# Second mixture of a two-layer gated kernel: from all experts for all tokens to rows scattered by expert

## The chip, the cores and the metric

The kernel runs on one core of one Trainium2 chip. The metric is device microseconds of one execution. A core has five engines that each follow a queue of their own and meet at semaphores: TensorE (PE, matrix products into PSUM banks), VectorE (DVE), ScalarE (ACT), GpSimd (POOL) and SyncE (SP, which only issues transfers). ScalarE and GpSimd issue transfers too, and an indirect transfer, whose row numbers come from a table in on-chip memory, is issued by GpSimd.

## The reference, cut to what matters

4096 tokens (64 batches of 64) of 128 values go through two layers. Each layer is a gated cross-attention and a gated mixture of experts:

```
x = x + tanh(g_xattn[0]) * attention0(layernorm(x), ctx, ...)
x = x + tanh(g_ffn[0])   * mixture0(layernorm(x), ...)      # 64 experts of 88, 8 per token, 2 shared
x = x + tanh(g_xattn[1]) * attention1(layernorm(x), ctx, ...)
x = x + tanh(g_ffn[1])   * mixture1(layernorm(x), ...)      # 8 experts of 512, 2 per token
```

The last line is the one that the change rewrites:

```
logits = xf @ Wg                                   # [4096, 8]
top_vals, top_idx = top_k(logits, 2)
gate_w = softmax(top_vals)
comb = sum(gate_w[..., None] * one_hot(top_idx, 8), axis=1)
for ei in range(8):
    hdd = gelu(xf @ W1[ei] + b1[ei])               # [4096, 512]
    y = hdd @ W2[ei] + b2[ei]                      # [4096, 128]
    out = out + comb[:, ei:ei+1] * y
```

All data are float32. Six of the eight weights of a token are zero, so a kernel may compute all eight experts for every token, or only the two that count.

## The kernel before, in words

The program has four stages, and every engine goes through them in the order `attention(0)`, `block_tables()` and `experts()`, `attention(1)`, `mixture(...)`. The order inside a stage is written out by hand.

**Attention** handles 16 groups of four batches (256 tokens, two tiles of 128) as a pipeline: in step j the group j is normalized and projected (`f`), group j-1 gets its scores (`m`), j-2 its values (`v`), j-3 its output projection and residual (`b`), j-4 its routing logits and ranks (`r`), j-5 its routing weights or row numbers (`k`). VectorE takes the maxima, the ranks and the residual, ScalarE the exponentials and the copies out of PSUM, GpSimd the inverse standard deviations (`deviation`, L1553). In layer 1 the routing ends with a table of weights `rw`, turned by TensorE (L599) and kept by ScalarE as `rwT` (L857); the normalized tokens are kept turned as `xn2T` (L910). Step 20 of layer 1 (`late`) runs inside the mixture, after chunk 10 of its first group.

**The first mixture** is sparse already. During attention(0) GpSimd scatters each token's row eight times into a table in DRAM (`expert_rows`), in a section per expert (L1516). TensorE counts the rows of each expert (L611 to L617), and `block_tables` makes the list of blocks of 128 rows: which expert and which rows a block takes. Everything is in two halves of 16 tiles. `experts` does 16 batches for the shared experts and 96 batches of four blocks: SyncE loads four blocks of rows (L409, three buffers), TensorE turns them (L674), multiplies by gate and up weights at an address from a register (L690), ScalarE applies silu, VectorE the product, TensorE turns the hidden values (L699) and multiplies down (L712), ScalarE copies the result (L963) and stores it to `expert_results` in DRAM (L967). GpSimd gathers eight result rows per token (L1531), and VectorE adds them into `x`, one scaled addition each (L1458). The first half's gathers run beside the second half's blocks; the second half's 128 gathers run in attention(1), ten a step, in front of and behind the deviations.

**The second mixture** is dense. It goes through eight groups of 512 tokens, and for each through 32 chunks of 128 hidden units (`group`, L766). Each float32 operand is split in two float32r parts, high and rest, and a product is three matmuls (`split_product`, L735: lines L739, L740, L741). Per chunk: ScalarE makes the high part of the weights (L1000) and GpSimd the rest (L1548); TensorE multiplies up (three matmuls of 512 columns) and spreads the token's weight for this expert over the 128 partitions (L781); ScalarE applies the gelu (L1029); VectorE multiplies by the spread weight (L1491); ScalarE and VectorE split the hidden values (L1007, L1472); TensorE multiplies down, three chunks later (three matmuls of 512 columns), adding up all 32 chunks in one bank. Behind a group, ScalarE copies the sum (L1013), TensorE turns it (L763), VectorE adds it to `x` (L1478) and SyncE stores 512 tokens (L443).

## Time and profile before

| | |
|---|---|
| median of three runs | 1671.78 us (1669.03 to 1679.33) |
| the profiled execution | 1676.6 us |
| its span, first to last instruction | 1674.8 us |
| TensorE busy | 1477.2 us, 88% of the span |
| VectorE, ScalarE, GpSimd busy | 1003.3, 913.8, 827.7 us |
| mean granted TensorE clock | 0.859 of full |
| moved by DMA | 129.98 MB |

The page has the share of busy time of each engine, the same in 40 slices with the granted clock, the chain of work that ended last, and the costliest groups of instructions by line. In such a row, `L712 PE MATMUL bank<-wexp,arena 88*128 x768 | 111.5, 291 | 53.1 <-...` means: line 712, TensorE, what it writes and reads, 768 records, busy for 111.5 us together, 291 ns each on the mean, and 53.1 us of idle time in front of them. A timeline row has the start and the duration in us, the engine, the line, and in brackets the idle time before and what ended it. In a row of stretches each engine has its busy time and its number of instructions.

### The profile page before, as it was taken

Reading aid. Unit: us, or ns where it says so; the run is one execution under the profiler, and the core shown is the slowest. Engines: PE = TensorE matmul, PEld = TensorE weight load, DVE = VectorE, ACT = ScalarE, POOL = GpSimd, SP = SyncE. Lnnn points to the kernel's source line nnn. Section 1 sums busy time; section 2 is a strip of 40 time slices with the busy share of each in tenths; the row PEclk is TensorE's granted clock in tenths of the full one; section 3 lists DMA queues with packets and bytes.
Section 4 is the critical chain, followed back from the end, with each engine's and each line's share of the span. In section 5 each row is a group of like instructions: output and inputs, shape, how many; then the busy total and the mean of one; then the engine's idle time right before and its main releaser. Section 6 shows DMA issues by size and latency. Waiting matters only on the chain. (4 is left out here: it accounts for less than half of the span.)

```text
span 1674.8 us, 30515 instructions
## 1 busy us (share of the span) xinstructions
PE 1477.2 (88%) x9346; PEld 1082.5 (65%) x9346; DVE 1003.3 (60%) x2799; ACT 913.8 (55%) x1981; POOL 827.7 (49%) x910
## 2 busy tenths in 40 slices
PE   4889887698767989966889899979999999999998
PEld 3666665488767988854666666645565565655655
DVE  4677876655334876653555555345666676666666
ACT  3666662245323555535444454446776776777776
POOL 1046667607785377767555540023444444444442
PEclk9999995799778999987655665558999999999999
DMA  6346541426443577753221110000000000000000
GB/s 166 84 111 180 175 143 45 126 83 197 146 137 120 169 212 206 205 157 106 75 68 43 43 41 7 1 0 1 8 1 7 1 6 6 0 7 0 6 7 7
DMA packets 210981, 129.98 MB, mean 78 GB/s; under 512 B 50882, under 2 KB 197378, under 8 KB 210834
## 3 DMA queue, kind: packets, MB, share of 16 engines
q1 hardware_dynamic: 139122, 60.97, 13.3%
q10 hardware_dynamic: 55296, 33.56, 6.8%
q0 software_dynamic: 16416, 33.65, 6.7%
q8 instruction: 72, 1.18, 0.3%
q14 instruction: 75, 0.61, 0.1%
HBM read 67.28 MB, written 60.82 MB: 76 GB/s over the span
## 5 line engine op out<-in xcount | busy, mean ns | idle before, releaser
L1548 POOL TENSOR_TENSOR wring<-weights,wring 128x256 fp32r<-128x256 f32 x256 | 240.8, 941 | 315.7 <-ACT wring L1000 315.7
L1516 POOL DMA_INDIRECT expert_rows<-xn2T,slot x256 | 253.3, 990 | 85.7 <-issue 80.0
L1472 DVE TENSOR_TENSOR hsplit<-work,hsplit 128x512 fp32r<-128x512 f32 x256 | 177.1, 692 | 126.1 <-ACT hsplit L1007 125.4
L1007 ACT ACTIVATE hsplit<-work 128x512 fp32r<-128x512 f32 x256 | 161.2, 630 | 144.9 <-PE bank L741 143.4
L1491 DVE TENSOR_TENSOR work<-work,bank 128x512 f32<-128x512 f32 x256 | 176.0, 687 | 68.5 <-ACT work L1029 52.7
L1029 ACT ACTIVATE work<-bank,b 128x512 f32<-128x512 f32 x256 | 171.5, 670 | 10.4 <-PE bank L741 9.7
L712 PE MATMUL bank<-wexp,arena 88*128 x768 | 111.5, 291 | 53.1 <-DVE arena L1377 52.7
L1531 POOL DMA_INDIRECT late_rows<-expert_results,slot x128 | 124.3, 971 | 59.2 <-issue 35.3
L848 ACT ACTIVATE work<-bank 128x512 f32<-128x512 f32 x128 | 76.5, 598 | 139.6 <-PE bank L507 136.9
L690 PE MATMUL bank<-wexp,arena 128*128 x768 | 147.2, 338 | 0.0
L1531 POOL DMA_INDIRECT xn2T<-expert_results,slot x128 | 121.9, 952 | 38.9 <-issue 38.9
L712 PEld LDWEIGHTS bank<-wexp,arena 88*128 88x128 f32 x768 | 99.8, 203 | 60.4 <-issue 60.3
L739 PE MATMUL bank<-hsplit,wring 128*128 128x512 f32 x256 | 131.9, 515 | 0.9 <-DVE hsplit L1472 0.8
L1555 POOL TENSOR_SCALAR ve<-mv 128x2 f32<-128x2 f32 (+1 forms) x52 | 11.8, 227 | 241.6 <-DVE mv L1143 155.7
L955 ACT ACTIVATE arena<-bank 128x176 f32<-128x176 f32 x224 | 70.1, 317 | 111.7 <-PE bank L690 78.5
L781 PE MATMUL bank<-xin,sel 16*128 16x512 f32 x256 | 130.1, 508 | 0.0
L690 PEld LDWEIGHTS bank<-wexp,arena 128*128 128x128 f32 x768 | 125.0, 204 | 7.3 <-issue 2.3
L507 PE MATMUL bank<-cst,work 128*128 128x128 f32 x512 | 106.7, 345 | 25.6 <-ACT sg L906 17.3
L963 ACT ACTIVATE arena<-bank 128x512 f32<-128x512 f32 x96 | 57.3, 597 | 114.3 <-PE bank L712 84.1
L1377 DVE COPY arena<-bank 88x512 f32<-88x512 f32 x112 | 76.5, 683 | 66.0 <-PE bank L699 65.9
L520 PEld LDWEIGHTS bank<-vm,work 128*64 128x64 f32 x2048 | 89.7, 171 | 36.2 <-ACT work L848 21.2
L781 PEld LDWEIGHTS bank<-xin,sel 16*128 16x128 f32 x256 | 48.1, 188 | 98.0 <-DVE work L1491 72.9
(197 smaller groups left out, 3204.9 us busy)
## 6 DMA issues: line engine op xcount, KB each, us to landing
arena<-expert_rows SPq DMA_DIRECT2D x384, 64.0 KB
expert_results<-arena ACTq DMA_DIRECT2D x96, 256.0 KB
expert_rows<-zero SPq DMA_DIRECT2D x256, 64.0 KB
arena<-in_ctxT ACTq DMA_DIRECT2D x32, 256.0 KB, 2.7
expert_rows<-xn2T,slot POOLq DMA_INDIRECT x256
weights<-in_mix SPq DMA_DIRECT2D x8, 512.0 KB
wexp<-in_mix SPq DMA_DIRECT2D x15, 176.0 KB
x<-in_x SPq DMA_DIRECT2D x4, 512.0 KB, 7.8
```

The lines of the kernel that those rows point to most:

```text
L507: mm = pe.transpose(w[:, bb * P:(bb + 1) * P], work[:, u, bb * P:(bb + 1) * P], ident)
L690: mm = pe.matmul(out[:, b * 2 * I0:(b + 1) * 2 * I0], xgT[:, n % 2, 2 * h + b, :], wflat[:, bass.ds(offsets[m][2 * h + b], 2 * I0)], start ...
L712: mm = pe.matmul(bank[7][:, b * P:(b + 1) * P], hT[0:I0, n % 2, b, :], wflat[0:I0, bass.ds(offsets[m][b] + 2 * I0, P)], start=True, stop=T ...
L739: pe.matmul(out, wh, xh, start=start, stop=False, skip_group_check=True)
L781: pe.matmul(bank[4 + c % 2][:, :], sel[strip, cols:cols + P], xin[strip, u, 2, :], start=True, stop=True).then_inc(S["spread"], 1)
L1007: act.activation(hsplit[:, c % 2, 0, :], work2[:, c % 2, :], ACT.Copy).then_inc(S["h_hi"], 1)
L1029: act.activation(work[:, c % 2, :], bank[c % 2][:, :], ACT.Gelu_apprx_tanh, bias=b1[:, c:c + 1]).then_inc(S["act"], 1)
L1472: dve.tensor_tensor(hsplit[:, c % 2, 1, :], work2[:, c % 2, :], hsplit[:, c % 2, 0, :].bitcast(F32), ALU.subtract).then_inc(S["h_lo"], 1)
L1491: dve.tensor_tensor(held, work[:, c % 2, :], bank[4 + c % 2][:, :], ALU.mult).then_inc(S["hid"], 1)
L1516: pool.indirect_dma_start(xs, bass.IndirectOffsetOnAxis(ap=slot[:, t, k:k + 1], axis=0), xn2all[:, t, :].bitcast(I32), None).then_inc(s_sc ...
L1531: pool.indirect_dma_start(yg[h][:, t // 2 % 2, t % 2, k, :].bitcast(I32), None, ys, bass.IndirectOffsetOnAxis(ap=slot[:, t, k:k + 1], axis ...
L1548: pool.tensor_tensor(wsplits[:, place, 1, 0:CW[1]], weights[:, c * CW[1]:(c + 1) * CW[1]], wsplits[:, place, 0, 0:CW[1]].bitcast(F32), ALU ...
```

## The change

The second mixture is built like the first. What it does, part by part:

- Routing of layer 1 keeps, for each token, which expert is first and which is second (`chosen`) and their two weights (`wk1`, times the gate). TensorE ranks the rows by expert (`rank_rows`, now in both layers), and VectorE makes the row number in the table (`slot1`). The turned weights and the turned tokens are no longer made; the normalized tokens are kept as rows.
- GpSimd scatters each token's row twice (`scatter_late`, 64 indirect transfers) during attention(1), after the gathers of the first mixture.
- SyncE loads the weights with the bias columns beside them, fills unused rows with zeros, and loads 20 batches of four blocks.
- `late_experts`: 80 blocks of 128 rows. VectorE copies a block's up weights and bias to a ring of four places; TensorE makes four plain fp32 products up into one bank; ScalarE applies four gelus of 128 columns; TensorE makes four plain fp32 products down, two blocks later; VectorE adds the bias of the output for four blocks at once; ScalarE stores them.
- GpSimd gathers two rows per token (`gather_late`, 64 indirect transfers), VectorE adds them into `x`, and SyncE stores 512 tokens at a time.
- All 21 steps of attention(1) come before the mixture.

The diff, cut to its core (tables, zero fills and declarations are left out):

```diff
 # SyncE
 def load_mixture():
-    part = CHUNKS[1] * CW[1] // 8
-    for i in range(8):
-        sp.wait_ge(layers[1]["vp"], i + 1)
-        sp.dma_start(weights[:, i * part:(i + 1) * part], A["mix1"][...]).then_inc(s_ffw, 16)
+    for e in range(E1):
+        sp.wait_ge(layers[1]["vp"], e + 1)
+        for a, at in ((0, 0), (1, W2C)):
+            sp.dma_start(wx[:, e, at:at + F1]..., mixed1[:, e, :, a, :]).then_inc(s_ffw, 16)
+    ...
+def load_late_rows(m):
+    if m >= XR:
+        sp.wait_ge(l_xt, m - XR + 1)
+    rows[m] = registers(sp, tabR1, m * NB, NB, (ROWS1 - P) * D)
+    for b in range(NB):
+        sp.dma_start(xg1[:, m % XR, b, :].bitcast(I32), flat1[bass.ds(rows[m][b], P * D)]...).then_inc(s_load[m % XR], 16)
 # TensorE
-if k and L: back_weights()
-if k and L == 0: rank_rows()
+if k: rank_rows()
 ...
-def mixture(step):
-    ...
+def late_experts():
+    def up(i):
+        m = i // NB
+        if i % NB == 0:
+            pe.wait_ge(l_xtc, m + 1)
+            offsets[m] = registers(pe, tabW1, m * NB, NB, (E1 - 1) * W1ROW)
+        pe.wait_ge(l_wc, i + 1)
+        if i > 2:
+            pe.wait_ge(l_act, i - 2)
+        for c in range(FC):
+            mm = pe.matmul(bank[2 + i % 3][:, c * P:(c + 1) * P], wcopy[:, i % WRING, c * P:(c + 1) * P], xgT1[:, m % 2, i % NB, :], ...)
+        mm.then_inc(l_up, 1)
+    def down(i):
+        m, b = i // NB, i % NB
+        pe.wait_ge(l_act, i + 1)
+        if b == 0 and m > 1:
+            pe.wait_ge(l_yc, m - 1)
+        for c in range(FC):
+            mm = pe.matmul(bank[5 + m % 2][:, b * P:(b + 1) * P], hT1[:, i % WRING, c, :],
+                           wxflat[:, bass.ds(offsets[m][b] + (W2C + c * P), P)], start=c == 0, stop=c == FC - 1, ...)
+        mm.then_inc(l_y, 1)
+    turn_rows(0)
+    for i in range(NBLOCKS1):
+        up(i)
+        if i % NB == 1 and i // NB + 1 < RT1:
+            turn_rows(i // NB + 1)
+        ...
+        if i > 1: down(i - 2)
+    down(NBLOCKS1 - 2)
+    down(NBLOCKS1 - 1)
 # ScalarE
-if r and L: keep_xn2()
-if k and L: keep_weights()
+    def gelus(i):
+        act.wait_ge(l_up, i + 1)
+        if i >= WRING:
+            act.wait_ge(l_y, i - WRING + 1)
+        for c in range(FC):
+            a = act.activation(hT1[:, i % WRING, c, :], bank[2 + i % 3][:, c * P:(c + 1) * P], ACT.Gelu_apprx_tanh,
+                               bias=wcopy[:, i % WRING, F1 + c:F1 + c + 1])
+        a.then_inc(l_act, 1)
 # VectorE
+    def copy_weights(i):
+        ...
+        if b == 0:
+            offsets[m] = registers(dve, tabW1, m * NB, NB, (E1 - 1) * W1ROW)
+        if i >= WRING:
+            dve.wait_ge(l_act, i - WRING + 1)
+        dve.tensor_copy(wcopy[:, i % WRING, :], wxflat[:, bass.ds(offsets[m][b], W1C)]).then_inc(l_wc, 1)
+    def keep_rows(m):
+        dve.wait_ge(l_y, (m + 1) * NB)
+        if m >= YR:
+            dve.wait_ge(s_store[m % YR], STORED[1][m % YR] + m // YR * 16)
+        for b in range(NB):
+            a = dve.tensor_tensor(yb1[:, m % YR, b, :], bank[5 + m % 2][:, b * P:(b + 1) * P], wxflat[...], ALU.add)
+        a.then_inc(l_yc, 1)
+    for i in range(3):
+        copy_weights(i)
+    for i in range(NBLOCKS1):
+        ...
+        if i + 3 < NBLOCKS1: copy_weights(i + 3)
+        ...
+        if i % NB == NB - 1: keep_rows(i // NB)
+        if i >= BLOCKS1 + 6 and i % 2 == 0 and (i - BLOCKS1 - 6) // 2 < HTILES:
+            combine((i - BLOCKS1 - 6) // 2)
+    for t in range(HTILES, TILES):
+        combine(t)
 # GpSimd
+def gather_late(i):
+    t, k = i // TOPK1, i % TOPK1
+    h = t // HTILES
+    if i == 0:
+        pool.wait_ge(s_comb, TILES * TOPK0)
+    if i % (HTILES * TOPK1) == 0:
+        pool.wait_ge(l_place, GROUPS + (h + 1) * 4)
+        for u in range(YR):
+            pool.wait_ge(s_store[u], STORED1[h][u])
+    if k == 0 and t > 3:
+        pool.wait_ge(l_comb, (t - 3) * TOPK1)
+    pool.indirect_dma_start(yg1[:, t % 4 * TOPK1 + k, :].bitcast(I32), None, ys1, ...slot1y[:, t, k:k + 1]...)
 ...
-for j in range(GROUPS + 3):
+for j in range(STEPS):
     if j < GROUPS:
         deviation(layers[1], "varp", "rstd", j, ...)
+    for part in range(2):
+        if fetched < TILES * TOPK0:
+            ...
+        else:
+            ready = max(j - LAGS + 1, 0) * 2 * TOPK1
+            for i in range(sent, min(sent + EARLY, ready)):
+                scatter_late(i)
+            sent = max(sent, min(sent + EARLY, ready))
+        if part == 0 and 3 <= j < GROUPS + 3:
+            deviation2(layers[1], j - 3)
-mixture()
+for i in range(sent, TILES * TOPK1):
+    scatter_late(i)
+for i in range(TILES * TOPK1):
+    gather_late(i)
```

## Rows read from the trace of the kernel before

**Rows 1.** The page, part 1: busy us, share of the span, instructions

```profile
PE 1477.2 (88%) x9346; PEld 1082.5 (65%) x9346; DVE 1003.3 (60%) x2799; ACT 913.8 (55%) x1981; POOL 827.7 (49%) x910
```

**Rows 2.** The page, part 4: the chain that ended last, by line

```profile
PE bank L739 4%; PE bank L740 3%; PE bank L741 3%; PE bank L781 2%; PE bank L751 0%; PE bank L763 0%; ACT ysb L1013 0%; DVE hsplit L1472 0%; ACT wring L1000 0%; DVE work L1491 0%; ACT hsplit L1007 0%; DVE x L1478 0%; ACT work L1029 0%; ACTq L1006 0%; ACTq L1028 0%
```

**Rows 3.** Stretches: PE, PEld, DVE, ACT, POOL busy (count), clock, DMA share, GB/s

```profile
815.00:1032.00 217.00, 190.63 (x1501) 141.04 (x1500) 118.06 (x437) 103.39 (x249) 101.09 (x125) 0.60 0.16 46
...
1110.00:1120.00 10.00, 9.32 (x17) 4.95 (x18) 3.69 (x6) 5.61 (x10) 5.30 (x6) 0.50 0.00 1
...
1150.00:1160.00 10.00, 10.00 (x37) 6.05 (x36) 6.67 (x10) 7.72 (x16) 4.49 (x5) 1.00 0.00 1
...
1200.00:1300.00 100.00, 99.45 (x339) 60.31 (x338) 66.18 (x97) 73.33 (x146) 43.45 (x47) 0.97 0.02 6
```

**Rows 4.** The page, part 5, one group

```profile
L739 PE MATMUL bank<-hsplit,wring 128*128 128x512 f32 x256 | 131.9, 515 | 0.9 <-DVE hsplit L1472 0.8
```

**Rows 5.** Groups by shape, 1250 to 1550 us: busy us, mean ns, idle before

```profile
L1029 ACT ACTIVATE work<-bank,b 128x512 f32<-128x512 f32 x140 | 93.7, 670 | 3.5 <-PE bank L741 3.1
```

**Rows 6.** Timeline (start us, us): first and last matmul of the dense mixture

```profile
1110.68 0.77 PE L739 MATMUL bank<-xin,wring 128*128 128x512 f32 x1 [4.67 <-DVE xin L1467]
...
1669.51 0.40 PE L741 MATMUL bank<-hsplit,wring 128*128 128x512 f32 x1
```

**Rows 7.** Timeline, TensorE: fp32 matmuls at full clock, then at half

```profile
206.99 1.11 PE L557 MATMUL bank<-wv,arena 128*128 128x128 f32 x8
...
661.83 0.60 PE L674 MATMUL bank<-cst,arena 128*128 128x128 f32 x4
...
662.27 1.06 PE L712 MATMUL bank<-wexp,arena 88*128 x8
...
663.16 0.60 PE L699 MATMUL bank<-cst,arena 128*88 128x128 f32 x4
...
1043.86 2.06 PE L557 MATMUL bank<-wv,arena 128*128 128x128 f32 x8
...
1045.84 1.05 PE L520 MATMUL bank<-vm,work 128*64 128x18 f32 x16
```

**Rows 8.** Groups by shape, 350 to 770 us

```profile
L712 PE MATMUL bank<-wexp,arena 88*128 x768 | 111.5, 291 | 53.1 <-DVE arena L1377 52.7 <-issue 0.3
...
L1377 DVE COPY arena<-bank 88x512 f32<-88x512 f32 x101 | 68.9, 683 | 64.8 <-PE bank L699 64.8
```

**Rows 9.** Stretches of 20 us in the first mixture, columns of rows 3

```profile
480.00:500.00 20.00, 11.75 (x68) 10.96 (x67) 6.29 (x13) 5.23 (x12) 15.96 (x17) 0.78 0.46 139
...
560.00:580.00 20.00, 20.00 (x159) 19.35 (x159) 16.43 (x34) 12.06 (x27) 6.79 (x7) 1.00 0.63 178
...
660.00:680.00 20.00, 18.07 (x141) 17.11 (x139) 12.84 (x34) 10.97 (x24) 15.12 (x17) 1.00 0.75 209
```

**Rows 10.** Groups by shape, 780 to 1110 us, second attention

```profile
L857 ACT ACTIVATE rwT<-bank 16x256 fp32r<-16x256 f32 x15 | 5.5, 368 | 6.1 <-PE bank L599 5.9
...
L1112 DVE TENSOR_TENSOR arena<-bank,rden 128x128 f32<-128x128 f32 x32 | 9.3, 291 | 1.1
...
L1261 DVE CAST rwr<-wsel 128x16 fp32r<-128x16 f32 x16 | 2.6, 165 | 0.1
```

**Rows 11.** Timeline, VectorE and GpSimd at work together

```profile
1108.46 3.94 POOL L1548 TENSOR_TENSOR wring<-weights,wring 128x256 fp32r<-128x256 f32 x5 [6.29 <-ACT wring L1000]
...
1108.57 0.65 DVE L1266 COPY rw<-rwr 128x16 f32<-128x16 f32 x1
```

**Rows 12.** Timeline, last gather of the first mixture and the combine behind it

```profile
741.87 0.94 POOL L1531 DMA_INDIRECT xn2T<-expert_results,slot  x1 [0.30 <-issue]
...
745.10 3.06 DVE L1458 SCALAR_TENSOR_TENSOR x<-xn2T,wk,x 128x128 f32<-128x128 f32 x8 [2.04 <-DMA xn2T<-expert_results,slot]
```

**Rows 13.** Timeline, end of the kernel

```profile
1671.29 0.75 DVE L1478 SCALAR_TENSOR_TENSOR x<-bank,gates,x 128x512 f32<-128x512 f32 x1 [2.40 <-PE bank L763]
...
1672.07 0.37 SPq L443 DMA_DIRECT2D out<-x  x1
```

598 lines of the change are left out of this document (305 added, 293 removed).

## The prediction

> **What bounds the kernel now.** I read the totals first [rows 1]: TensorE is busy for 88% of the span, the others for 49 to 60%. That is an average over four stages, so I looked at the stretches next [rows 3] and at the first and last matmul of the dense mixture [rows 6]. The mixture runs from 1110.7 to 1669.5 us, a third of the kernel, and in 1200 to 1300 us TensorE is busy 99.45 of 100 us. The chain that ended last [rows 2] is shared out among that mixture's four matmul lines (L739, L740, L741, L781); it was followed back for a tenth of the span only, but it names the same engine as the stretch. The mixture does 256 chunks [rows 4], each of seven matmuls of 512 columns, so one takes 558.8/256 = 2.18 us. VectorE, ScalarE and GpSimd have a third or more of this stage free: only removing matmul time shortens it. The second attention before it is bound by TensorE too (190.6 of 217 us busy, at a granted clock of 0.60) and hardly changes.
>
> **What the change removes.** All 256 chunks with their splits, the 558.8 us between the two rows [rows 6], and the small work behind them up to the last addition (1671.3 us [rows 13]). The last attention step, until now done inside the first chunks, comes back to the end of the attention.
>
> **Start of the new stage.** The last routing operation of before ends at 1108.57 + 0.65 = 1109.2 us [rows 11]. Behind it now stand the last step's placing of rows, four VectorE operations of 0.17 us [rows 10] with their waits (about 0.8 us), the read of four offsets into registers (no row of VectorE shows one; between 0 and 1.2 us, I take 1) and the first weight copy. The copy is 516 columns, SBUF to SBUF. Nearest is the 512-column copy from PSUM, 683 ns [rows 8]: I take 0.7. The first up matmul starts at about 1112 us, which is 1.3 us later than the first dense one.
>
> **TensorE per block.** Up is four matmuls of 128 rows by 128 columns in plain fp32, down four more, and each block has one transpose. An fp32 matmul is two records in the trace (768 for 384 [rows 8]). At full clock four of them, with register addresses, run from 662.27 to 663.16: 0.89 us; another four are busy for 1.11 us with their drain [rows 7], so four cost 0.9 to 1.1 us. Four transposes go from 661.83 to 662.27: 0.11 us each. A block is 2 x 0.95 + 0.11 = 2.0 us; bounds 1.9 and 2.3. 80 blocks: 160 us (152 to 184). At half clock four take 1045.84 - 1043.86 = 1.98 us, so a block takes 2 x 1.98 + 0.22 = 4.2 us.
>
> **Clock.** In the second attention the granted clock is 0.60, and the dense mixture's opening ran at half clock (0.50 in 1110 to 1120) though TensorE had hardly a gap; it read 1.00 from 1150 to 1160 on [rows 3]. I price the same opening for the new stage: some 45 us (1110.7 to about 1155) at half clock, worth about 22 us at full. The first mixture shows the other end: busy at full clock from its first batches (0 us). I take 22, since the work ahead of this stage is that of the dense row. Short dips as in 1200 to 1300 (0.97) add 3% of 110 us, 3 us.
>
> **The other engines beside it.** ScalarE, per block: four gelus of 128 columns. The 512-column gelu takes 670 ns [rows 5], a 256-column copy without bias 368 ns [rows 10]. A line through the two gives 0.22 us for 128 columns, too low because the second has no bias; 0.37 is the upper end. I take 0.35, near the 256-column row. So 0.9 to 1.5 us, a quarter of a 512-column copy (0.15) and of a store's issue (0.1): at most 1.75, below 2.0. VectorE: weight copy 0.69, bias addition 0.29 [rows 10], later two combines at 3.06/8 = 0.38 for every second block [rows 12]: 1.4 us, below 2.0. Its queue has one tight place: keep_rows waits for a batch's fourth down product, and the copy for the block after next stands behind it. That costs 4 x 0.29 + 0.69 = 1.85 us and two hand-overs, while TensorE has one up and one down left, 1.9 us. I charge 0.5 us for each of 20 batches: 10 us (bounds 0 and 80, the second being the register reads and combines in the same gap, 4 us a batch). SyncE: 20 batches of four row loads. The first mixture did a batch in about 3.1 us in its good stretches and in 5 to 6 where loads and scatters met (11.75 of 20 us busy in 480 to 500, against 20.00 in 560 to 580 [rows 9]); the new batch lasts 8 us, so the loads are covered, and if that cover failed it would be at the first batch of the second half alone, which waits for the 64th scatter. Those rows are wanted 40 blocks after it.
>
> **The weight copy against a rule.** The rows have a small sign of VectorE and GpSimd disturbing each other: the copy at L1266 took 0.65 us while GpSimd worked [rows 11], against 0.165 for its neighbour of the same width [rows 10]. The Trainium skill (VectorE: DVE Perf Modes, What auto-detection actually checks) says that a copy with one source, SBUF to SBUF, runs two elements a cycle; by that the copy would be about 0.35 us, an estimate from that page, and the 10 us of stalls would go to nearly 0. No row shows such a copy at this width, so the sum keeps 0.7.
>
> **GpSimd's queue.** Its 256 weight subtractions go. In the second attention 64 scatters come, ten a step from step 13 on, then four a step as groups are ranked, each 0.94 + 0.30 = 1.24 us [rows 12]. Behind them are queued the two small inverse deviations for which VectorE and then ScalarE wait. Ten cost 12.4 us in a step of some 20, and steps 0 to 12 already carry ten gathers; I price 0 (at most 10 us, in the shorter draining steps). The first half's 32 gathers (40 us) run beside the second half's blocks (80 us): 0. If that cover went, they would join the tail.
>
> **Second attention.** Per step: ScalarE loses two copies of 0.4 us, TensorE swaps two transposes for four short bf16 products, VectorE gains about four operations of 0.17 us. Over 16 steps that lies between -12 and +13 us, and TensorE sets the pace: 0. SyncE's weight loads (16 of 256 KB for 8 of 512 KB, nine small ones) and 32 zero fills fall where it is idle. One more table of 66 KB at the start: under 1 us.
>
> **The tail.** Nothing hides the second half's gathers: they need every result row stored. Behind the last down product: bias additions 4 x 0.29 = 1.2; the store of 256 KB, as the last output store from 1672.07 to the span's end at 1674.8, 2.8; 32 gathers of 1.24, 39.7; landing of the last, 745.10 - 742.81 = 2.3; two combines 0.8; output store 2.8 [rows 12, 13]. Together 49.6 us, against 5.3 between last product and end of before.
>
> **Sum.** 1112 + 160 + 22 + 3 + 10 = 1307 us for the last product, + 49.6 = 1357 us of span. The profiled execution took 1676.6 us for a span of 1674.8, so 1.8 more: 1359. It was 4.8 us above the median of 1671.78; the same share off gives **1355 us**, 19% less.
>
> **Rivals.**
> - Half clock throughout, as in the attention, where TensorE is 88% busy and gets 0.60. Four-row hand-overs could leave such gaps. Against it: 0.97 to 1.00 in the first mixture at 90% busy [rows 9]. Then 80 blocks at 4.2 us, 336 for 182: 1355 + 150 = 1505 us. Chance 0.10.
> - VectorE's queue becomes the bound: the stall of 4 us a batch above, + 70: 1425 us. For it: three kinds of wait in one queue. Chance 0.14.
> - Gathers held up by the weight copies. A gather that has to wait for each copy would take 1.24 + 0.7, or, where it loses twice, 2.6 us or more; 32 of them then last 85 us and, begun some 10 us into the second half's 80, end 15 us after its last block: 1370 us. Rows 11 show a copy slowed, no row a gather. The Trainium skill (SBUF — State Buffer) calls this pair of ports an exclusive lock and gives 3.1 us for such a DMA against 0.62 alone; by that figure the 32 last about 99 us, an estimate. Chance 0.06.
> - Slower than before: the blocks run one after the other, because the ring of copied weights frees a place only when a gelu is done and the copies stand behind keep_rows. A block then costs its whole chain at half clock: copy 0.7, up 2.0, gelus 1.5, down 2.0, addition 0.3, hand-overs 0.3 = 6.8 us; 1112 + 544 + 50 = 1706 us. It decides from (1672 - 1112 - 50)/80 = 6.4 us a block. Against it: four places in the ring and a down product two blocks behind its up. Chance 0.03.
>
> **Chances and range.** The forecast has 0.67. Its own range: down to 1310 (clock opening, stalls and 8 us of matmul bound gone, attention 5 better), up to 1400 (matmuls 24 more, attention and scatters 20). The range is 1310 to 1450: it takes in the VectorE and gather rivals and leaves out the half clock and the serial case. A measurement of this kernel tells 1% from no change: faster 0.96, same 0.01, slower 0.03.
>
> **What would show it.** First up matmul near 1112 us; first to last product about 195 us; TensorE over 90% busy there with a clock of 1.00 after the opening; idle before the up matmuls put down to VectorE's copies under 1 us a batch; a bare run of 32 gathers of 1.24 us each at the end, with TensorE idle for 50 us. Wrong would be: a granted clock of 0.5 deep in the stage, blocks of 3 us, gathers over 1.3 us, or an attention that ends more than 15 us elsewhere.

## The result, and the profile after

The changed kernel takes 1301.34 us (median of 4 runs, 1299.05 to 1315.93), the kernel before beside it 1675.55 us (1669.03 to 1686.86): a ratio of 0.778, 95% interval 0.771 to 0.785. It is 22% faster. I had said 1355 us, with 1310 to 1450 around it, so the kernel gained more than I gave it, and lay below my range. Medians here are over all timed runs of a kernel; the ratios leave out runs that fell in a slower state of the chip. The profiled execution took 1302.38 us for a span of 1300.6, against the sum's 1357.

The page's totals and the start of its chain of waits:

```profile
PE 1050.2 (81%) x8918; PEld 892.8 (69%) x8918; DVE 720.4 (55%) x2590; ACT 604.6 (46%) x1497; POOL 710.9 (55%) x781
...
PE 44%; POOL 27%; DVE 12%; issue 11%; ACT 4%; DMA 1%; SPq 0%; POOLq 0%; DVEq 0%; ACTq 0%
```

TensorE lost 427 us of work against [rows 1] and the span 374. The chain now has GpSimd in it for 27%: the gathers behind the last product are one part of that. Groups of the page (busy us, mean ns of one, idle before and its releaser): the up products (L794), the gelu, the gathers, and the attention's score products.

```profile
L794 PE MATMUL bank<-xgT,wcopy 128*128 128x128 f32 x640 | 86.0, 279 | 1.1 <-DVE wcopy L1512 1.1
...
L1004 ACT ACTIVATE arena<-bank,wcopy 128x128 f32<-128x128 f32 x320 | 91.5, 369 | 51.5 <-PE bank L794 51.5
...
L1620 POOL DMA_INDIRECT late_rows<-expert_results,slot1y x64 | 61.9, 967 | 129.5 <-DMA expert_results<-yb 99.7
...
L552 PE MATMUL bank<-cst,work 128*128 128x128 f32 x512 | 102.9, 335 | 39.2 <-ACT sg L925 30.8
```

The 1.1 us that TensorE waited for a weight copy stand in front of the very first up product; between the first product and the last it waited for nothing (I had charged 10 us for stalls on VectorE's queue). The stretches, with the columns of [rows 3]:

```profile
748.00:1091.00 343.00, 277.42 (x2406) 212.28 (x2406) 186.08 (x735) 157.83 (x369) 208.96 (x248) 0.65 0.23 65
...
1093.00:1096.00 3.00, 2.54 (x12) 2.56 (x13) 1.25 (x4) 1.77 (x4) 2.39 (x3) 0.50 0.41 130
1097.00:1100.00 3.00, 3.00 (x28) 2.87 (x26) 1.73 (x8) 2.67 (x9) 2.18 (x3) 1.00 0.29 92
...
1120.00:1200.00 80.00, 80.00 (x718) 79.88 (x717) 28.17 (x98) 53.41 (x179) 13.77 (x15) 1.00 0.31 88
1200.00:1240.00 40.00, 40.00 (x361) 40.00 (x361) 19.36 (x65) 26.50 (x90) 17.95 (x18) 1.00 0.37 104
...
1260.00:1300.00 40.00, 0.00 (x0) 0.00 (x0) 9.85 (x28) 0.00 (x0) 24.53 (x26) 0.50 0.26 71
```

Three things are to be seen. The granted clock goes from 1.2 to 2.4 GHz at 1096.6 us, 3 us behind the first product; in the dense mixture it did so at 1146.7 only, 36 us behind its own first product. From 1120 to 1240 TensorE is busy for every microsecond at full clock. And from the last product to the end it does nothing. The timeline of TensorE (start and duration in us), the opening and a batch:

```profile
1093.46 3.51 PE L794 MATMUL bank<-xgT,wcopy 128*128 128x128 f32 x16 [1.06 <-DVE wcopy L1512]
...
1152.57 1.06 PE L804 MATMUL bank<-wx,arena 128*128 x8
1153.46 1.06 PE L794 MATMUL bank<-xgT,wcopy 128*128 128x128 f32 x8
1154.36 1.06 PE L804 MATMUL bank<-wx,arena 128*128 x8
1155.25 1.06 PE L794 MATMUL bank<-xgT,wcopy 128*128 128x128 f32 x8
1156.14 1.06 PE L804 MATMUL bank<-wx,arena 128*128 x8
1157.04 1.06 PE L794 MATMUL bank<-xgT,wcopy 128*128 128x128 f32 x8
1157.93 0.60 PE L782 MATMUL bank<-cst,xg 128*128 128x128 f32 x4
```

Four products start 0.89 us after the four before them, up and down alike, so a block is 1.79 us and every fourth, with its batch's turning, 2.22: 1.90 on the mean (I had 2.0). The end, VectorE, ScalarE's queue and GpSimd:

```profile
1248.11 0.89 DVE L1519 TENSOR_TENSOR yb<-bank,wx 128x128 f32<-128x128 f32 x4 [3.48 <-PE bank L804]
1249.02 0.37 ACTq L1010 DMA_DIRECT2D expert_results<-yb  x1
1252.79 0.95 POOL L1620 DMA_INDIRECT late_rows<-expert_results,slot1y  x1 [20.17 <-DMA expert_results<-yb]
1254.04 0.94 POOL L1620 DMA_INDIRECT late_rows<-expert_results,slot1y  x1 [0.30 <-issue]
...
1291.48 0.94 POOL L1620 DMA_INDIRECT late_rows<-expert_results,slot1y  x1 [0.30 <-issue]
...
1293.91 0.74 DVE L1547 SCALAR_TENSOR_TENSOR x<-late_rows,wk,x 128x128 f32<-128x128 f32 x2 [1.66 <-DMA late_rows<-expert_results,slot1y]
1294.68 0.37 SPq L488 DMA_DIRECT2D out<-x  x1
```

The last product ends at 1248.0, the store's landing lets the first of 32 gathers go at 1252.8, they leave every 1.25 us, and the output store is the last thing, 5.9 us from its issue to the span's end. The whole tail is 52.6 us (49.6 predicted).

### The profile page after: what moved, and what is told of

The parts are those of the page before. It is cut to its first block, busy times and chain, and to the rows that moved or that the text cites. A ratio compares the mean times of both kernels' runs of the same rounds, so it can differ in the third digit from the quotient of the medians.

```text
span 1300.6 us, 28093 instructions
## 1 busy us (share of the span) xinstructions
PE 1050.2 (81%) x8918; PEld 892.8 (69%) x8918; DVE 720.4 (55%) x2590; ACT 604.6 (46%) x1497; POOL 710.9 (55%) x781
## 3 DMA queue, kind: packets, MB, share of 16 engines
q8 instruction: 77, 1.26, 0.4%
## 4 chain that ended last, share of the span: by engine, by line
PE 44%; POOL 27%; DVE 12%; issue 11%; ACT 4%; DMA 1%; SPq 0%; POOLq 0%; DVEq 0%; ACTq 0%
POOL expert_rows L1578 9%; POOL xn2T L1593 9%; PE bank L794 6%; PE bank L804 6%; PE bank L552 4%; PE bank L565 4%; POOL late_rows L1593 3%; DVE x L1497 2%; PE bank L620 2%; PE bank L619 2%; POOL late_rows L1620 2%; PE bank L736 2%; PE bank L530 2%; PE bank L581 2%; DVE arena L1100 2%
## 5 line engine op out<-in xcount | busy, mean ns | idle before, releaser
L552 PE MATMUL bank<-cst,work 128*128 128x128 f32 x512 | 102.9, 335 | 39.2 <-ACT sg L925 30.8
L1620 POOL DMA_INDIRECT late_rows<-expert_results,slot1y x64 | 61.9, 967 | 129.5 <-DMA expert_results<-yb 99.7
L1004 ACT ACTIVATE arena<-bank,wcopy 128x128 f32<-128x128 f32 x320 | 91.5, 369 | 51.5 <-PE bank L794 51.5
L1408 DVE TENSOR_TENSOR arena<-arena,bank 128x176 f32<-128x176 f32 x224 | 72.2, 334 | 63.5 <-ACT arena L967 62.4
L565 PEld LDWEIGHTS bank<-vm,work 128*64 128x64 f32 x2048 | 85.6, 164 | 31.1 <-ACT work L872 20.4
L552 PEld LDWEIGHTS bank<-cst,work 128*128 128x128 f32 x512 | 68.6, 167 | 49.4 <-issue 46.2
L565 PE MATMUL bank<-vm,work 128*64 128x18 f32 x2048 | 98.8, 233 | 4.2 <-ACT work L872 3.9
L1085 DVE TENSOR_REDUCE nmax<-bank 128x8 fp32r<-128x512 f32 x128 | 85.3, 673 | 14.6 <-PE bank L536 9.6
L794 PE MATMUL bank<-xgT,wcopy 128*128 128x128 f32 x640 | 86.0, 279 | 1.1 <-DVE wcopy L1512 1.1
L581 PE MATMUL bank<-arena,wqk 128*128 128x256 f32 x192 | 66.1, 459 | 24.0 <-DVE arena L1100 11.4
```

The lines of the kernel that those rows point to most:

```text
L552: mm = pe.transpose(w[:, bb * P:(bb + 1) * P], work[:, u, bb * P:(bb + 1) * P], ident)
L565: mm = pe.matmul(w2[b2 * SEQ:(b2 + 1) * SEQ, at:at + 2 * VW], work2[:, u % 2, pair * P + b2 * SEQ:pair * P + (b2 + 1) * SEQ], vm[:, V % 3, ...
L581: mm = pe.matmul(w[:, h * GTOK:(h + 1) * GTOK], wqk[:, n, h * P:(h + 1) * P], rhs, start=True, stop=True)
L794: mm = pe.matmul(bank[2 + i % 3][:, c * P:(c + 1) * P], wcopy[:, i % WRING, c * P:(c + 1) * P], xgT1[:, m % 2, i % NB, :], start=True, sto ...
L1004: a = act.activation(hT1[:, i % WRING, c, :], bank[2 + i % 3][:, c * P:(c + 1) * P], ACT.Gelu_apprx_tanh, bias=wcopy[:, i % WRING, F1 + c: ...
L1085: dve.tensor_reduce(nmax[:, u, :], score[u][:].rearrange("p (a k) -> p a k", k=SEQ), AX.X, ALU.max, negate=True).then_inc(S["max_done"], 1)
```

## The experiments

Three questions came out of the comparison of the two traces. Why does the clock rise at once? My first theory was that plain fp32 products leave TensorE no gaps; when `dense_plain` spoke against it, the next was that the new stage has no product of 16 rows among those of 128. Why is attention 2 shorter: because the removed copies and transposes were on its path, or in those executions only? And is the tail one queue of gathers, or is it set by the gathers of the second part alone? Each kernel gives one profile; some were timed in several runs, and then the ratio to the kernel before on the same chip has its interval. Those without an interval ran once.

### The tail: parts of 22 and 10, 24 and 8, 20 and 12 tiles instead of 16 and 16

The row tables, block lists and transfers of layer 2 are in two parts; these kernels move the border, so that fewer gathers are left for the end (`PARTS`, `BST` replace the halves everywhere in layer 2):

```diff
+TST = [0, 20, TILES]                       # 22, 24 in the others
+BST = [0, NT1[0] * TOPK1 + E1, TILES * TOPK1 + 2 * E1]
-if i == BLOCKS1 - NB:
+if i == BST[1] - NB:
-sp.wait_ge(s_scat[h], HTILES * (TOPK0 + TOPK1) * 16)
+sp.wait_ge(s_scat[h], (HTILES * TOPK0 + NT1[h] * TOPK1) * 16)
```

> The second mixture's two parts are 22 and 10 tiles of tokens instead of 16 and 16 (52 and 28 blocks; 44 and 20 gathers), the combines of the first part one every 1.25 blocks. Theory: the 52.6 us behind the last product are the second part's gathers, 32 at 1.25 us, that nothing hides. With 20 of them left, and the first part's 44 (55 us) beside 28 blocks (54 us), the tail is 52.6 - 12 x 1.25 = 38 us plus some 1 to 6 us by which the first part's gathers end late: the kernel is 9 to 14 us faster than with halves, about 1290 us. Rival: the tail is set by the stores' landing and the final additions, not by the number of gathers; then no change. Second rival: the denser gathers and combines beside the blocks hold up VectorE's weight copies, and TensorE shows idle time before the up products; then less than 5 us.

> Parts of 24 and 8 tiles (56 and 24 blocks; 48 and 16 gathers). If the gathers are one queue at 1.25 us each, the first part's 48 (60 us) no longer fit beside 24 blocks (46 us), end some 18 us behind the last product, and 16 more follow: last gather about 38 us behind the last product, some 6 us later than with 22 tiles, and still some 8 us earlier than with halves. If not the queue but the number of gathers of the last part set the tail, it would be shorter than with 22 tiles, near 33 us.

> Parts of 20 and 12 tiles (48 and 32 blocks; 40 and 24 gathers). With 22 tiles the first part's gathers began 9 us behind its last block, took 1.31 us each beside the blocks, and 28 instead of 20 were left behind the last product: tail 42.2 us. With 20 tiles the first part's 40 take 52 of 62 us and are done in time, and 24 are left: 24 x 1.25 + 5 for the store + 7 = 42 us, against 52.6 with halves. So about 10 us faster than the changed kernel run beside it, and the same as with 22 tiles. Rival: the tail's gain is eaten up beside the blocks, since the first part ends later: no change.

| kernel | first product | to last product | gathers behind it | tail | time |
|---|---|---|---|---|---|
| 16 and 16 (changed kernel) | 1093.5 | 154.5 | 32 | 52.6 | 1301.34 |
| the same, other chip | 1108.4 | 155.9 | 32 | 52.3 | 1312.67 |
| 20 and 12 | 1100.9 | 158.3 | 24 | 41.4 | 1304.32 |
| 22 and 10 | 1100.4 | 158.1 | 28 | 42.2 | 1307.2 |
| 24 and 8 | 1105.6 | 157.7 | 34 | 49.6 | 1314.72 |

I had expected 22 and 10 to be 9 to 14 us faster than halves, near 1290 us. It isn't: its ratio to before is 0.777 (0.773 to 0.781), that of halves 0.778. With 22 and 10 the second part has 20 gathers, and yet 28 stand behind the last product; with 24 and 8 it has 16, and 34 do. The gathers are one queue. With 22 and 10 the first part's 44 begin at 1211.4 us, 5.7 us behind that part's last product, and leave every 1.31 us, so they need 57.5 us, and only 47.2 us are left to the last product of all. Moving the border pays until the first part's gathers reach past the last product. At 20 and 12 they are just done. The timeline there, where only the second part's 24 are left:

```profile
1259.34 0.88 DVE L1526 TENSOR_TENSOR yb<-bank,wx 128x128 f32<-128x128 f32 x4 [0.72 <-PE bank L811]
1260.26 0.37 ACTq L1017 DMA_DIRECT2D expert_results<-yb  x1
1263.51 0.94 POOL L1626 DMA_INDIRECT late_rows<-expert_results,slot1y  x1 [7.34 <-DMA expert_results<-yb]
```

GpSimd idled 7.34 us there, so the first part's gathers had ended. The tail is 10.9 us shorter than on the same chip with 16 and 16, the stretch of products 2.4 us longer. On that chip the medians are 1304.32 (ratio 0.773, 0.769 to 0.778) and 1312.67 (0.778, 0.774 to 0.782): 8.4 us apart by the medians, which is the tail's 10.9 less the products' 2.4, but with intervals that overlap (of the 36 pairs of one run of each, 33 have 20 and 12 ahead). The profile shows where the gain comes from; the runs alone do not settle its size. It is the fastest version against before that I ran, and by the intervals not surely so.

### The changed kernel again, five rounds

> The changed kernel once more, beside the run with another split, and for a second look at its second attention. In four looks at kernels with the changed attention it lasted 343 to 361 us from its first projection to the first up product, longer with a lower granted clock (0.649 to 0.580). Theory: the 17 us by which the changed kernel's mixture started earlier than the dense one were mostly the clock of that one profile; this look then starts its mixture anywhere between 1093 and 1108 us. Rival: the change shortens the attention by 17 us; then the start is at 1093 us again at whatever clock.

It took 1312.67 us (1302.95 to 1318.42), before 1688.4, a ratio of 0.778. The ratio came back to within a thousandth, the time is 11 us more, before's 13. The 1312.67 us are inside the range that I had given. Its first product started at 1108.4 us with a granted clock of 0.586 in attention 2, against 1093.5 and 0.649 in the profile above. So a good part of the early start above comes from the clock that the chip granted and not from the change. It was no matter of the profiled execution alone: over the whole kernel the mean clock was 0.839 to 0.845 in three of the four runs behind 1301.34 us, and 0.819 to 0.834 in the six behind 1312.67.

### Attention 2: putting its removed work back

The first kernel lets TensorE turn two 16-row strips a step again, the second lets ScalarE do its two copies again; both write where nobody reads. The transposes wait for `q_read` as they did before; the copies' waits are left out here:

```diff
+if k and L:                                   # attention_products
+    if f:
+        pe.wait_ge(S["q_read"], F + 1)
+    for t in range(2):
+        pe.transpose(w0[0:2 * E1, t * P:(t + 1) * P], cst[:, 0:2 * E1], ident)
...
+if r and L:                                   # attention_copies
+    act.activation(filler[:, 0:GTOK], ysb[:, 0:GTOK], ACT.Copy)
+if k and L:
+    act.activation(filler[0:2 * E1, 0:GTOK], cst[0:2 * E1, 0:GTOK], ACT.Copy)
```

> The changed kernel with two fp32 transposes of 16 columns by 128 put back on TensorE in each step of the second attention that ranks rows (their result is used by nobody). They took 0.57 us a step at half clock. Theory: TensorE sets the attention's pace, so 16 steps get 5 to 9 us longer at the same granted clock. Rival: what the change saved there was ScalarE's copies; then nothing changes. Read at the granted clock of the stretch, since the clock alone moves it by some 18 us between looks.

> The changed kernel with ScalarE's two copies per step put back in the second attention (256 columns, 0.38 and 0.37 us; their result is used by nobody). Theory: ScalarE is busy less than half of that stretch and the copies fall where it idles: within 3 us of the changed kernel at the same granted clock. Rival: TensorE waits for ScalarE's copies out of PSUM there, and 0.75 us a step costs up to 12 us.

The span of attention 2 (its first projection to the first product of the mixture) has to be read against its granted clock, since that differs from one execution to the next:

| kernel | granted clock | length, us | above the line |
|---|---|---|---|
| changed kernel | 0.649 | 343.3 | -1.6 |
| the same, other chip | 0.586 | 357.0 | -2.0 |
| 20 and 12 | 0.621 | 352.1 | +0.9 |
| 22 and 10 | 0.617 | 351.0 | -1.1 |
| 24 and 8 | 0.595 | 358.3 | +1.3 |
| before | 0.599 | 362.2 | +6.1 |
| with the transposes back | 0.644 | 356.5 | +10.4 |
| with the copies back | 0.645 | 353.5 | +7.7 |

The line is fitted through seven kernels with the changed attention (the five above and two further down): 490.2 us less 224 times the clock, none of them over 2.5 us off. The kernel before lies 6 us above it, and so does the dense kernel without spreading (+6.3); the dense one with plain products is 13.0 above. Either piece put back brings the stage to where before was or above. So the change does shorten attention 2, by 6 to 13 us at equal clock, and neither piece is hidden. The three dense kernels have the same attention and lie 7 us apart, and each piece was put back in one execution only, so their sizes are rough. They don't add up to the difference, so how it is shared between them stays open. For the transposes the waits of TensorE show the path. In before (L599) and with them put back (L675) they wait for VectorE; the changed kernel has no such wait (engine line waited for: us in total, times, longest us):

```profile
PE bank L599 <- DVE arena L1131: 7.4, 11, 0.7
...
PE bank L675 <- DVE arena L1117: 6.4, 11, 0.6
```

For the copies the row is L552 above: TensorE waits 30.8 us there behind ScalarE's `sg`, the routing logits. ScalarE's queue, in which the copies stood, is on the path of this stage; I had priced it as covered because TensorE is 88% busy. The size of that wait doesn't show the copies' share: it was 24 to 31 us in kernels with the changed attention, 17 and 25 us in dense ones, and 33.6 us with the copies back.

### VectorE's queue: each weight copy made twice

```diff
+dve.tensor_copy(wcopy[:, i % WRING, :], wxflat[:, bass.ds(offsets[m][b], W1C)]).then_inc(l_wc2, 1)
+dve.wait_ge(l_wc2, i + 1)
 dve.tensor_copy(wcopy[:, i % WRING, :], wxflat[:, bass.ds(offsets[m][b], W1C)]).then_inc(l_wc, 1)
```

> Every block's up weights are copied twice by VectorE, one copy behind the other, 80 copies more. The changed kernel shows 0.43 us a copy where I had taken 0.7 and charged 10 us of TensorE stalls. Theory: VectorE has slack of about 0.6 us at the tight place (bias additions 0.8 + two copies 0.9 against 1.9 us of TensorE work), so doubling the copy costs under 5 us in all. Rival: the tight place is as tight as the prediction said, then 20 batches lose about 0.3 to 0.5 us each, 6 to 10 us, and idle time before the up products is put down to the copies.

1315.75 us, ratio 0.781 (0.775 to 0.786); from first to last product 161.9 us instead of 154.5 to 155.9. The copy is 0.43 us, so two of them make up about what I had priced for one (0.7) and more. The timeline of one batch's boundary:

```profile
1199.99 0.89 DVE L1522 TENSOR_TENSOR yb<-bank,wx 128x128 f32<-128x128 f32 x4 [3.69 <-PE bank L805]
1200.46 0.97 PEld L805 LDWEIGHTS bank<-wx,arena 128*128 128x128 f32 x8
1200.57 1.06 PE L805 MATMUL bank<-wx,arena 128*128 x8
...
1200.79 0.42 DVE L1513 COPY wcopy<-wx 128x516 f32 x1
1201.24 0.53 DVE L1515 COPY wcopy<-wx 128x516 f32 x1
...
1201.83 1.16 PE L795 MATMUL bank<-xgT,wcopy 128*128 128x128 f32 x8 [0.20 <-DVE wcopy L1515]
```

The up products start 1.26 us behind the down products instead of 0.89. This is the tight place of my sum, where keep_rows stands ahead of a copy, and it costs 0.37 us in most batches, 20 x 0.37 = 7 us. That is what this run's rival said and not its theory of under 5 us. The mechanism is right, and there is little room: in the changed kernel the copy at this place ends 0.25 us before its product starts, here 0.06 us, so 0.2 us are to spare, and it costs nothing.

### What holds the clock down, and what a dense chunk costs

Five kernels take the difference between the two mixtures apart. One gives the dense mixture one plain fp32 product in place of three and so leaves out the two correction products, one leaves its spreading product out but for the first two chunks (the token weights are then missing from the result), one puts a spreading pair of 16 rows in the sparse one, whose result is overwritten:

```diff
-pe.matmul(out, wh, xh, ...)                     # dense_plain: one fp32 product in place of three
-pe.matmul(out, wh, xl, ...)
-return pe.matmul(out, wl, xh, ...)
+return pe.matmul(out, wh.bitcast(F32), xh.bitcast(F32), start=start, stop=stop, ...)
...
+if first(g, 0) and c < 2:                       # dense_no_spread
     pe.matmul(bank[4 + c % 2][:, :], sel[strip, cols:cols + P], xin[strip, u, 2, :], ...)
...
+for c in range(2):                              # sparse_with_spread; sparse_full_rows: 0:16 left out
+    pe.matmul(bank[2 + i % 3][:, 0:P], wcopy[0:16, i % WRING, 0:P], xgT1[0:16, m % 2, i % NB, :], ...)
```

> The kernel before, with the dense mixture's three float32r products replaced by one plain fp32 product of the high parts (it leaves out the two correction products; everything else stays). It asks whether the kind of product decides how long the mixture's opening stays at half clock. Theory: the new stage got the full clock within about 5 us because plain fp32 products leave TensorE no gaps, where the float32r chunks had gaps between matmuls at half clock; then this run's opening is at full clock within about 10 us too. Rival: the opening of 45 us at half clock belongs to this place in the program or to chance; then it stays at half clock for tens of us here as well. A chunk should take 2 x 0.85 us and the spreading product, about 2.1 us, at full clock.

1743.2 us, 55 more than the kernel before beside it (1688.21); the clock rose 25.4 us behind the first product. The sparse mixture is not fast because of its plain products, and they are not what lets the clock rise at once.

> The kernel before without the product that spreads the token's weights over the partitions (L781, 16 rows by 512 columns), but for the first two chunks; VectorE multiplies by what the bank holds. It asks what kept the dense mixture's opening at half clock: 36 us in the kernel before, 25 us with plain fp32 products, 3 to 6 us in the new stage. Theory: the 16-row product and the gaps on either side of it; then the full clock comes within about 10 us of the first chunk. Rival: the float32r products themselves, or the place; then 25 us or more again. At full clock a chunk should be 0.36 to 0.5 us shorter, about 1.7 us, unless ScalarE (0.67 + 0.63 + 0.40 = 1.70 us a chunk) holds it there.

1526.24 us where before took 1694.37 beside it. The rise came after 15.2 us; the first two chunks still had their product of 16 rows. Six products of 512 columns a chunk now start every 0.23 us; the stretch of 1300 to 1400 has ScalarE at 93.34 of 100 us, so another engine has come near, and a chunk takes 1.60 us.

> The changed kernel with two plain fp32 products of 16 rows by 128 columns put in front of each block's up products (their result is overwritten). Theory: if products that use 16 rows delay the rise of the clock, the new stage's opening is now longer at half clock than the 3 to 6 us of four looks. Rival: no effect on the opening. Either way each block gets 0.45 to 0.6 us longer, 80 of them some 36 to 48 us: TensorE bounds the stage.

1385.98 us (before beside it 1694.37); 230.2 us from first to last product, 0.94 us a block more than the changed kernel, and the rise 25.4 us behind the first product. Its stretches, before and after that:

```profile
1101.00:1126.00 25.00, 25.00 (x103) 22.19 (x103) 2.10 (x9) 6.71 (x23) 5.48 (x6) 0.50 0.13 40
1128.00:1200.00 72.00, 72.00 (x555) 65.25 (x554) 18.33 (x68) 32.66 (x110) 0.00 (x0) 1.00 0.20 58
```

TensorE has no idle time in the first 25 us and is held at 1.2 GHz all the same. That speaks against gaps as the reason. Two products of 16 rows brought back both marks of the dense mixture: the late rise and a price beyond their columns. The rival was the products themselves, whatever their rows. The last two kernels use all 128 rows, each on two chips; in the dense one the added rows of weights and pattern are zero:

```diff
-strip, cols = slice(0, 2 * E1), c // (F1 // P) * P     # dense_full_rows
+strip, cols = slice(0, P), c // (F1 // P) * P
+dve.memset(xin[:, :, 2, :].bitcast(F32), 0.0).then_inc(s_zx, 1)
```

> The kernel before, whose spreading product (L781) now uses 128 rows (the table and the weights are padded with zeros; same columns, same result) instead of 16. Without that product a chunk took 1.60 us and the clock rose 15 us after the first chunk; with it 2.02 us at full clock and 36 us. Theory: what costs is the change between 16-row and 128-row products, not the product's 512 columns; then a chunk takes 7 x 0.23 = 1.61 to 1.75 us (ScalarE needs 1.70), the stage 410 to 460 us for 559, the kernel is 6 to 9% faster than before, and the clock rises within about 15 us. Rival: the product costs the same with 128 rows; then no change.

> The counterpart in the changed kernel: the two extra products in front of each block's up products use 128 rows instead of 16. With 16 rows a block got 0.94 us longer (230.2 us for the stage against 154.5 to 155.9) and the clock rose 25 us after the first product instead of 3 to 6. Theory: the change of rows costs; now each block gets only 2 x 0.23 = 0.45 us longer, the stage takes about 192 us, and the clock rises within 6 us. Rival: extra products cost 0.94 us a block whatever their rows, 230 us.

> The kernel before with the spreading product fed with all 128 rows of the weights and of the spreading pattern (zeros in the other rows) in place of 16; same result. It ran once on a chip whose first mixture was 300 us longer: there the clock rose 3.5 us after the first dense product and the dense stage took about 444 us, against 35.9 us and 557 us in the kernel before on another chip. Theory (switching between 16 and 128 rows delays the clock's rise and costs about 0.4 us a chunk): the stage is 440 to 450 us again, the rise comes within 10 us, and the time is 105 to 125 us below the kernel before of the same chip, near 1560 to 1585 us where before takes 1680. Rival (the earlier chip made both): the rise comes 25 us or more behind the first product and the gain is under 60 us.

> The changed kernel with the two spreading products of a block put back, fed with 128 rows; it ran once on the slower chip with a stage of 200.9 us (0.58 us a block over the changed kernel's 154.5) and the clock's rise 4.4 us after the first product; with 16 rows it was 230.2 us and 25.4 us. Theory: stage 199 to 203 us again, rise within 7 us, time near 1350 us (changed kernel's 1305 plus 46). Rival (the chip): stage 220 us or more and a rise behind 20 us.

Both chips were slower in the stages ahead, so the times that I had expected of the second (1560 to 1585 and 1350 us) did not come: there the kernel before took 2039.63 and 2011.38 us, and attention 2 began at 1067 and 1051 us instead of 750. I read the last stage alone, and the ratios. In the kernels with a pair, rise and length are counted from the first up product, about 1 us behind the pair:

| kernel | clock's rise behind the first product | first to last product | time, ratio to before |
|---|---|---|---|
| before (16 rows) | 36 us | 559.2 | 1 |
| dense, 128 rows | 3.4 us | 440.7 | 1906.08, 0.937 (0.928 to 0.947) |
| the same, other chip | 3.4 us | 440.6 | 1886.8, 0.942 (0.932 to 0.952) |
| changed kernel (no such product) | 3.1 us | 154.5 | |
| sparse, 16-row pair | 25.4 us | 230.2 | 1385.98 |
| sparse, 128-row pair | 4.3 us | 200.9 | 1733.58 |
| the same, other chip | 3.1 us | 199.2 | 1700.04 |

With 128 rows both marks are gone, in both mixtures and on both chips. One rival stays for the clock: all four profiles with 128 rows are of the two chips that were slower ahead, and no kernel with 16 rows was profiled there. Those chips granted no more in attention 2 (0.55 to 0.60), but that the early rise there comes from the rows is not shown as firmly as that 16 rows delay it in the sparse mixture (3 to 6 us without the pair, 25.4 with it). For the price of the product the chip is no rival: the ratios are to before on the same chip, and the steps below are the same without that product on a chip of the other kind.

The timeline of TensorE shows where the time lies. First before, one chunk of the dense mixture, with weight loads (PEld); then the same with 128 rows:

```profile
1250.92 0.40 PE L740 MATMUL bank<-xin,wring 128*128 128x512 f32 x1
1250.92 0.19 PEld L741 LDWEIGHTS bank<-xin,wring 128*128 128x128 f32 x1
...
1251.16 0.39 PE L741 MATMUL bank<-xin,wring 128*128 128x512 f32 x1
1251.48 0.18 PEld L781 LDWEIGHTS bank<-xin,sel 16*128 16x128 f32 x1 [0.36 <-DVE work L1491]
1251.48 0.49 PE L781 MATMUL bank<-xin,sel 16*128 16x512 f32 x1
...
1251.89 0.19 PEld L739 LDWEIGHTS bank<-hsplit,wring 128*128 128x128 f32 x1 [0.24 <-issue]
1251.90 0.51 PE L739 MATMUL bank<-hsplit,wring 128*128 128x512 f32 x1
```

```profile
1551.23 0.40 PE L743 MATMUL bank<-xin,wring 128*128 128x512 f32 x1
1551.23 0.19 PEld L783 LDWEIGHTS bank<-xin,sel 128*128 128x128 f32 x1
1551.46 0.40 PE L783 MATMUL bank<-xin,sel 128*128 128x512 f32 x1
1551.47 0.19 PEld L741 LDWEIGHTS bank<-hsplit,wring 128*128 128x128 f32 x1
1551.70 0.39 PE L741 MATMUL bank<-hsplit,wring 128*128 128x512 f32 x1
1551.93 0.39 PE L742 MATMUL bank<-hsplit,wring 128*128 128x512 f32 x1
```

Between products of 128 rows the weight load of the next (L741) starts with the product before it, 0.24 us ahead. At the change to 16 rows, and at the change back, the load starts with its own product (1251.48 and 1251.48, 1251.89 and 1251.90), so nothing hides it: steps of 0.32 and 0.42 us instead of 0.23, and 0.34 for the product behind. The bracket at L781 names a wait for VectorE; the program has the same wait in front of L783, and there the load goes 0.23 us ahead, so the wait isn't the reason. A chunk is 2.02 us (L781 at 1251.48 and 1253.50) with 16 rows, 1.62 with 128 (L783 at 1551.46 and 1553.08). 256 x 0.40 = 102 us, and 36 us of opening at half clock instead of 3.4 are 16 more: 118, where the stage shortened by 119, and the whole kernel on its own chips by 128 and 116 (the ratios' share of 2039.63 and 2011.38). In the sparse mixture, TensorE in a full stretch gets through

```profile
1200.00:1320.00 120.00, 120.00 (x925) 109.40 (x924) 35.12 (x118) 55.68 (x187) 31.80 (x32) 1.00 0.25 67
```

925 records in 120 us with 16 rows (7.7 a microsecond) and, with 128,

```profile
1500.00:1560.00 60.00, 60.00 (x540) 60.00 (x539) 16.56 (x57) 31.67 (x107) 4.27 (x5) 1.00 0.25 70
```

9.0 a microsecond. 21 records make a block in both, so that is 2.72 and 2.33 us, against 1.88 in the changed kernel (361 records in 40 us, 17 a block): the pair costs 0.84 us with 16 rows and 0.45 with 128. (The stage took 199 to 201 us with 128 rows and not the 192 expected, in part because TensorE idled for some 3 to 5 us around 1563 us on one chip and 1596 on the other, where it waited for nothing that the profile shows, and was granted 0.5 for 7 us behind that.) The Trainium skill (TensorE: Matmul & The Clock Gate, Step-by-step: what each phase is for) says that weight loads are pulled ahead of running products when the row groups don't conflict or the load goes to the background buffer, and that the row count does not matter for a load's duration. The trace agrees with the second (0.18 and 0.19 us) and shows what a load that isn't pulled ahead costs.

Not every change of the row count costs that. The first mixture of before goes from transposes of 128 rows to down products of 88 (L712) and back to 128 (L699), and there the loads start 0.11 us ahead of their products (662.27 and 663.16 [rows 7]):

```profile
662.16 0.97 PEld L712 LDWEIGHTS bank<-wexp,arena 88*128 88x128 f32 x8
...
663.05 0.46 PEld L699 LDWEIGHTS bank<-cst,arena 128*88 128x88 f32 x4
```

So the price is shown for 16 rows beside 128, not for 88; what lies between was not tried. For the clock no run shows more than the order of things: the stages that have products of 16 rows among those of 128 rise late (15 to 36 us), those that don't within 3 to 7. The latter holds for the first mixture too: it rose at 317.2 us, its first product being at 310.7, and stayed at 1.00 when its products of 88 rows began at 318.1.

## Why the prediction was off, by its own steps

| step | predicted | measured | difference |
|---|---|---|---|
| first product (attention 2) | 1112 | 1093.5 | -18.5 |
| clock's opening | 22 | 1.6 | -20.4 |
| dips of the clock | 3 | 0 | -3 |
| stalls on VectorE's queue | 10 | 0 | -10 |
| 80 blocks | 160 | 152.9 | -7.1 |
| tail | 49.6 | 52.6 | +3.0 |
| span | 1357 | 1300.6 | -56 |

(The block row is what is left of the 154.5 us, 1.91 us a block.) That TensorE bounds the stage, what a block costs and the bare tail of gathers were right, and none of the four rivals came: full clock instead of half, no bound on VectorE, gathers done in time, no serial blocks. The step that failed is the clock's opening, **"I price the same opening for the new stage ... I take 22, since the work ahead of this stage is that of the dense row"**. The new stage lost 1.6 us there, 3.1 us at half clock. What decided was the work in the stage, not the work ahead of it. The price itself was also read too high: before was at half clock for 36 us, not 45, which is worth 18 us and not 22. The traces had the sign: the first mixture ran at full clock from its first batches [rows 9], with products of 88 and 128 rows and none of 16, and the dense chunk had L781 with 16 rows at 509 ns beside five neighbours of 407 to 415 and the one behind it at 516. I read the first mixture as the other end of a range instead of asking which of the two the new stage resembles.

The second is **"Over 16 steps that lies between -12 and +13 us, and TensorE sets the pace: 0"**. It has two parts. At equal clock attention 2 is 6 to 13 us shorter, because ScalarE's copies and TensorE's transposes were on the path. The rest, about 10 us, is the granted clock (0.649; 0.580 to 0.626 in six other kernels with the same attention, whose first product lay at 1100 to 1108), and that was luck: on the other chip the same kernel took 1312.67 us, inside the range, for the same ratio of 0.778. The ratio of the forecast, 0.81, is off either way. For the range that mattered: its low end took 5 us off for the attention; with 12, and with the dips, it would have stood at 1300. A stage at a granted clock of 0.6 also moves by itself by 10 us, and no term had that.

The others are sizes. The weight copy took 0.43 us, not the 0.7 of a copy out of PSUM. By the rule weighed against the trace (the Trainium skill, VectorE: DVE Perf Modes, What auto-detection actually checks) I had estimated 0.35 and stalls of nearly 0: the measured copy is nearer to that than to 0.7, and on the stalls it was right. The tight place exists, as the doubled copy shows, with 0.2 us to spare. A block is 1.9 because four products are 0.89 and no drain stands between up and down. Gelus took 369 ns (0.35 taken), the bias additions 0.9 us together (1.2), both of no weight. In the tail the gathers left every 1.25 us as priced; the store's landing took 3.8 us instead of 2.8 and the output's 5.9 instead of 2.8, both larger than the last store of before, and the landing of the last gather 1.5 instead of 2.3.

The rival of gathers held up by copies: beside copies they left every 1.31 us (with parts of 22 and 10, some of that waiting for combines), alone every 1.25, and four of the 80 copies, beside a scatter or gathers, took 0.50 to 0.68 us instead of 0.43. Those four would fit the lock of the Trainium skill (SBUF — State Buffer, Who interferes with whom), though no run isolates it; the 3.1 us that it gives for a transfer (A bandwidth-pool intuition that's wrong) are not in this kernel, whose gathers are 967 ns on the mean.

Not settled: how attention 2's gain is shared between the two removed pieces; why two chips are slower ahead of the last stage; and whether the clock rises as early with 128 rows on a chip that isn't.

## What to carry to other kernels

Look at the rows of each product beside its duration: a product of 16 rows among products of 128 cost 0.40 us a chunk, and zeros in the other 112 rows make the dense kernel 6% faster. The clock's late rise was gone too, on the two chips where that was tried. When a new stage replaces another, take its clock from the stage whose products are like it, not from the one that stood in its place. And when a second half's gathers are left bare at the end, move the border: of the four tried, the shortest tail (41.4 us for 52.3) is where the queue of the first part's gathers just ends before the last product.

## What the runs showed of the hardware

- A product of 16 rows between products of 128: its weight load starts with the product itself, and the steps are 0.32 and 0.42 us instead of 0.23. A product of 88 rows between products of 128 has its load 0.11 us ahead and doesn't pay this (before, 662.16 us).
- TensorE without a gap for 25 us stays at 1.2 GHz when pairs of 16 rows stand among products of 128, and goes to 2.4 GHz in 3 to 6 us without them. With pairs of 128 rows, on other chips, it took 3 to 4 us.
- A copy of 516 fp32 columns within SBUF by VectorE: 0.43 us; one beside a scatter 0.68. Indirect gathers of 128 rows with nothing beside them leave every 1.25 us.
- The length of attention 2 follows its granted clock, 2.2 us less for 0.01 more, and that clock was 0.580 to 0.649 in kernels whose attention was the same. Two other chips lay 27 to 49 us above that line.
